# A mixture-of-experts feed-forward on one core: indirect scatters and gathers issued in pairs, each pair behind the landing of the pair ahead

## What is computed

```python
logits = jax.nn.relu(xf @ Wr1 + br1) @ Wr2 + br2
gates = jax.nn.softmax(logits, axis=-1)
tg, ti = jax.lax.top_k(gates, K)              # K = 2
tg = jax.nn.softmax(tg / K, axis=-1)
out = jax.nn.silu(xf @ Ws1 + bs1) @ Ws2 + bs2
for e in range(E):                            # E = 8
    h = jax.nn.silu(xf @ We1[e] + be1[e]) @ We2[e] + be2[e]
    w = jnp.sum(tg * (ti == e), axis=-1)
    out = out + w[:, None] * h
...
x = x + jnp.tanh(g_ffn[1]) * _L1_ffn_ref(_layernorm(x, axis=-1), ...)
```

## Time and profile before

| | |
|---|---|
| three timed runs | 319.92, 322.65, 322.99 us; median 322.65 us |
| the profiled execution, its own time | 319.63 us |
| its span (first to last instruction in the trace) | 317.9 us, so 1.7 us lie around it |
| mean granted TensorE clock | 0.946 |
| busy: PE, DVE, ACT, POOL | 84%, 61%, 49%, 30% |
| indirect DMAs: scatters (L652), gathers (L664) | 16 and 16 |

### The profile page before, as it was taken

How to read it: one execution, slowest core, us unless ns; L and a number is a source line. 1 busy time by engine, 2 the same in 40 slices (tenths; PEclk the granted TensorE clock), 3 DMA queues, 4 the chain that set the end, 5 groups by cost and what they waited for, 6 DMA issues and landing times.

```text
span 317.9 us, 6233 instructions
## 1 busy us (share of the span) xinstructions
PE 268.3 (84%) x2073; PEld 231.7 (73%) x2073; DVE 192.8 (61%) x614; ACT 154.9 (49%) x374; POOL 93.9 (30%) x140
## 2 busy tenths in 40 slices
PE   1998986989989988899999999586798975799960
PEld 0577855778868777798988997574788964799950
DVE  2789836688899975347777487865445730122232
ACT  3582466778876666213342441602559620356420
POOL 1265012578854341021002010550100720035053
PEclk9999999899999999989999999787799995999995
DMA  7799885000000000100000000066800148943132
GB/s 194 250 314 243 217 176 118 1 4 5 26 2 2 3 0 2 36 2 0 0 2 0 2 1 0 20 214 163 276 19 2 41 152 278 278 113 87 34 92 66
DMA packets 30847, 27.31 MB, mean 86 GB/s; under 512 B 2705, under 2 KB 24329, under 8 KB 30816
## 3 DMA queue, kind: packets, MB, share of 16 engines
q1 hardware_dynamic: 29408, 24.45, 26.7%
q0 software_dynamic: 1408, 2.46, 3.1%
HBM read 19.17 MB, written 7.73 MB: 85 GB/s over the span
## 4 chain that ended last, share of the span: by engine, by line
PE 52%; DVE 19%; issue 12%; POOL 8%; DMA 4%; SPq 3%; ACT 2%; POOLq 0%; DVEq 0%; ACTq 0%
PE bank L1386 12%; PE bank L1361 6%; PE bank L1373 5%; PE bank L1194 4%; PE bank L1196 4%; PE bank L1195 3%; PE bank L1179 3%; POOL p_sb L625 3%; DVE xhat_sb L895 3%; DVE sum_sb L832 3%; PE bank L1139 2%; DMA ctx_tok_sb<-in_ctx 2%; PE bank L1150 2%; POOL w_q_sb L664 2%; DVE x_sb L1119 2%
## 5 line engine op out<-in xcount | busy, mean ns | idle before, releaser
L779 ACT ACTIVATE p_sb<-bank,bias_t_sb 128x128 f32<-128x128 f32 x120 | 33.8, 374 | 32.5 <-PE bank L1361 32.4
L625 POOL TENSOR_TENSOR p_sb<-p_sb,recip_sb 128x480 f32<-128x480 f32 x32 | 31.6, 988 | 52.1 <-DVE recip_sb L835 52.1
L768 ACT ACTIVATE hT_sb<-bank,cols_sb 128x512 f32<-128x512 f32 x40 | 27.1, 690 | 40.5 <-PE bank L1196 40.3
L1373 PE MATMUL bank<-we_sb,p_sb 128*128 x240 | 32.3, 280 | 3.5 <-issue 3.5
L673 POOL TENSOR_TENSOR rstd_sb<-veps_sb,minus_half_sb 128x4 f32<-128x4 f32 (+1 forms) x11 | 10.6, 966 | 83.1 <-DVE veps_sb L887 82.9
L1386 PEld LDWEIGHTS bank<-w_sb,hT_sb 128*128 128x128 f32 x256 | 32.0, 200 | 2.1 <-issue 1.3
L1373 PEld LDWEIGHTS bank<-we_sb,p_sb 128*128 128x128 f32 x240 | 29.6, 195 | 4.9 <-issue 4.8
L1386 PE MATMUL bank<-w_sb,hT_sb 128*128 128x128 f32 x256 | 32.8, 284 | 0.0
L1119 DVE SCALAR_TENSOR_TENSOR x_sb<-bank,wts_sb,x_sb 128x128 f32<-128x128 f32 x64 | 18.0, 344 | 19.3 <-PE bank L1386 19.2
L652 POOL DMA_INDIRECT xs_hbm<-xhat_sb,slots_sb x16 | 15.7, 983 | 40.9 <-DVE slots_sb L809 36.7
L1150 PE MATMUL bank<-ident_sb,p_sb 128*120 128x128 f32 x128 | 20.2, 285 | 7.7 <-POOL p_sb L625 7.4
(11 more groups left out here) (221 smaller groups left out, 590.6 us busy)
## 6 DMA issues: line engine op xcount, KB each, us to landing
xs_hbm<-col_rows_sb SPq DMA_DIRECT2D x2, 2048.0 KB, 19.6
tile_w_sb<-in_L_ffn_We SPq DMA_DIRECT2D x15, 256.0 KB, 3.6
w_sb<-in_L_ffn_We SPq DMA_DIRECT2D x8, 256.0 KB, 4.0
w_after_sb<-in_L_ffn_We SPq DMA_DIRECT2D x7, 256.0 KB, 3.7
w_kv_sb<-in_L_xattn_w_kv SPq DMA_DIRECT2D x2, 512.0 KB, 6.6
w_sb<-in_L_ffn_w SPq DMA_DIRECT2D x1, 1024.0 KB, 10.9
xs_sb<-xs_hbm SPq DMA_DIRECT2D x15, 64.0 KB, 2.8
w_kv_sb<-xs_hbm SPq DMA_DIRECT2D x15, 64.0 KB, 2.9
```

Of the source, the lines that this page charges most:

```text
L625: nc.gpsimd.tensor_tensor(p0[j % 4], p0[j % 4], recip0[:, j % 2, :].unsqueeze(2) .broadcast_to([128, HG, SK]), ALU.mult).then_inc(probs_re ...
L768: nc.scalar.activation(hT[:, u % 2, c, :], ps(item)[:, :], ACT.Relu if n == 1 else ACT.Silu, bias=cols[:, col:col + 1]).then_inc(read(item ...
L779: last = nc.scalar.activation(hT_t[:, u % RING, c, :], ps(item)[:, 128 * c:128 * (c + 1)], ACT.Silu, bias=bias_t[:, p, c, j:j + 1])
L1373: last = nc.tensor.matmul(dst[:, 0:C], hT_t[:, slot, c, :], we2[:, bass.ds(e, 1), c, :].rearrange("p a h -> p (a h)"), start=(c == 0), sto ...
```

## The change

Two waits are added on POOL, and nothing else. In the scatter of block i > 0, POOL waits until the scatters of all blocks before it have landed. In the gather of block i > 0, POOL waits until both gathers of block i-1 have landed. Within a pair (k = 0, 1) nothing waits. That is 3 waits in each of the four sequences of 8 indirect DMAs.

```diff
@@ -648,6 +648,8 @@
                     if i == 0:
                         pool.wait_ge(slots_ready, p + 1)
                         pool.wait_ge(loaded["xs_clear"], 32)
+                    else:
+                        pool.wait_ge(scattered[p], 16 * 2 * i)
                     for k in range(2):
                         pool.indirect_dma_start(
                             out=xs_hbm[p], out_offset=bass.IndirectOffsetOnAxis(
@@ -660,6 +662,8 @@
                     for i in range(HB):
                         if p:
                             pool.wait_ge(gathered[i], 16 * 2)
+                        if i:
+                            pool.wait_ge(gathered[i - 1], 16 * 2 * (p + 1))
                         for k in range(2):
                             pool.indirect_dma_start(
                                 out=y_of[p][:, k, i, :], out_offset=None, in_=ys_hbm[p],
```

## The result

The changed kernel is slower: median 331.48 us over four runs (329.56 to 332.09) against 321.51 (319.92 to 322.99). The ratio is 1.030, 95% interval 1.023 to 1.038. The forecast was 330.4 in 325.0 to 335.5. A later series gave the same again: 330.71 against 321.88, ratio 1.030, interval 1.023 to 1.037.

What follows compares the result with a forecast made beforehand. A chain of waits bounds it, the last gather's landing delaying the end one for one. 5.4 + 2.3 + 1.6 = 9.3 gives 328.9 us from the profiled execution's 319.63, 332.0 from the median 322.65; middle 330.4, range 325.0 to 335.5.

Steps and rivals of the forecast that it cites:

- The tail: Half 1's gathers at the kernel's end: three waits delay the last gather and the end one for one, +5.4 us.
- the restart behind a landing: Time POOL needs to start its next DMA after a waited-for landing: taken as 0.5 us, ends 0.3 and 0.77.
- Half 0's start: Half 0's scatters: SP's row loads start 3.7 us later, less 2.05 of slack, so +1.6 us.
- The slack: At half 0's start, PE and DVE had other work, so 2.05 us of later rows would be hidden.
- Half 1's start: Half 1's scatters: SP waits 3.2 us longer, row loads land 0.9 faster, PE starts +2.3 us late.
- Half 0's gathers: Last gather issued 5.3 us later, but covered by DVE's later combine and 4.65 us idle behind it: 0.
- The clock: Rival, 0.11: each longer PE idle leaves one more block at half clock, 2 x 1.75 = +3.5 us.
- Only the tail shows: Rival, 0.14: the scatters' six waits are hidden, only half 1's gathers cost, +5.4: 325.0 or 328.1 us.
- Not slower: Rival, 0.02: POOL's 0.94 us per indirect DMA is queue back-pressure, so issues get shorter: 318.3 or 321.3 us.
- Waits that do nothing: Rival, 0.03: landings are over when POOL comes to the waits, so time as before.

Runs made afterwards that it cites:

- e1_gather1: Kernel before plus only the three waits between the pairs of half 1's gathers, two semaphores each: 331.81 us, ratio 1.018.
- f4_gather0_late: Kernel before with half 0's gathers, no waits between them, starting only when tile 8 of half 1 is copied out: 322.33 us, ratio 1.001.
- f3_gather0_again: Kernel before plus only the three waits between the pairs of half 0's gathers, run again on another chip: 322.74 us, ratio 1.002.
- f1_before: Kernel before, unchanged, run once more with a profile: 322.58 us, ratio 1.001.
- e3_scatter1: Kernel before plus only the three waits between the scatter pairs of half 1: 331.08 us, ratio 1.012.
- e7_gather1_each: Kernel before, each half 1 gather waiting for the one ahead, one semaphore each; waits for half 0's gathers moved ahead of all eight: 337.14 us, ratio 1.037.

## Why the prediction was right, point by point

**The tail: right place, mis-sized (+5.4, measured +6.7 and +6.4).** All of it reaches the end: DVE's last combine starts 2.5 to 2.6 us behind the last gather before and after. Alone it costs 1.8% (`e1_gather1`). The term that was off is the restart behind a landing: 0.5 was taken between the ends 0.3 and 0.77. It is 0.7 here, because these waits carry two semaphores, and 0.2 to 0.3 with one. The nearest row, 0.7 behind a store's landing, had the size; whether its three semaphores were the reason, as the prediction half suspected, was not tested apart. The other part is the first landing, 3.2 us (2.9 in the second profile) instead of 2.7: DMA issues at 310.70 us and then 315.86 us of the changed kernel:

```profile
w_q_sb<-ys_hbm,y_slots_sb POOLq DMA_INDIRECT x1, 3.2
...
w_q_sb<-ys_hbm,y_slots_sb POOLq DMA_INDIRECT x1, 2.5
```

**Half 0's start: right mechanism, too small (+1.6, measured +2.5).** The last scatter was predicted to land 3.7 us later, and SP's first row load came 3.9 later (17.66 us behind the first scatter instead of 13.77). The wait beside the weight loads was longer, 4.7 us instead of the 3.5 taken, and the restarts shorter, 0.2 to 0.3 instead of 0.5, which nearly cancels. What wasn't in the sum: the fourth row load took 2.6 us, not 1.8. DMA issues at 210.90 and at 221.04 us of the changed kernel:

```profile
xs_hbm<-xhat_sb,slots_sb POOLq DMA_INDIRECT x1, 4.7
...
xs_sb<-xs_hbm SPq DMA_DIRECT2D x1, 64.0 KB, 2.6
```

3.9 + 0.8 - 2.05 of slack = 2.65, against 2.5 measured. The slack, read from when PE and DVE would have been free, was right.

**Half 1's start: right, a little too large (+2.3, measured +1.6).** The restart was 0.3, so a step between pairs is 2.51 and not 2.7; the last landing took 3.4 as against 3.5 taken; SP was 2.5 late, not 3.2. That the row loads then land 0.9 us faster came true: 1.9 instead of 2.8. PE's idle grew from 5.18 to 6.72, where about 7.5 was expected.

**Half 0's gathers: right (0).** The last lands at 303.3 and DVE's combine starts at 306.54; `f4_gather0_late` shows that even 10.7 us are covered by the combine and the idle behind it.

**The clock: a rival by itself, in fact a part.** One microsecond lies behind half 1's first multiplications, and both profiles of the changed kernel have it. PE's timeline of the changed kernel, the next two tiles' worth behind 271.89:

```profile
273.74 1.92 PE L1377 MATMUL bank<-we_sb,p_sb 128*128 x8
275.44 1.70 PE L1365 MATMUL bank<-pT_sb,w_sb 128*128 128x128 f32 x8
276.97 1.06 PE L1377 MATMUL bank<-we_sb,p_sb 128*128 x8
```

In the kernel before the first two of these blocks took 1.56 and 1.06:

```profile
269.16 1.56 PE L1373 MATMUL bank<-we_sb,p_sb 128*128 x8
270.55 1.06 PE L1361 MATMUL bank<-pT_sb,w_sb 128*128 128x128 f32 x8
```

PE stood at 1.2 GHz (granted 0.50 in 272 to 276 us) for 1 us longer. But `f3_gather0_again`, with an idle of 5.70 us and none of the scatter waits, shows 1.92 and 1.82 as well, and `f1_before`, with 7.60 us, only 1.92 and 1.17, so the longer idle isn't shown to be the cause: when the clock comes back also varies between executions. At half 0's start nothing was added, the 16 matmuls took 3.58 us instead of 3.48. The prediction's "+1.75 for each" was too much.

**The rivals that fell.** Only the tail shows: no, half 0's and half 1's stages grew in both profiles of the changed kernel, and half 1's in `e3_scatter1` alone. Not slower, by quicker issues: an indirect DMA took 0.94 to 0.96 us of POOL behind a wait as before it (the first scatters of a sequence 1.0 to 1.1 in both kernels), and with one in flight in `e7_gather1_each` 0.94 to 1.00. Waits that do nothing: true only of waits two pairs back.

The terms' errors, +1.3, +0.9, -0.7 and the +1.0 of the clock, add up to 2.5 of the 3.0 us between 12.3 and 9.3; the rest is the 0.4 ahead of the first scatter and rounding. The time was still near the middle of the range since it started from halfway between the own time and the median.

That the forecast came so near is in part luck. The medians differ by 10.0 and 8.8 us, which the sum's 9.3 matches, while the stages grew by 11.9 us against an execution at the fast end. The terms were too small by about as much as that execution lay below the usual one. Where a usual execution of the kernel before spends the 2 to 3 us isn't settled. The stage to half 1's first gather may be the place: it took 36.6 us in the first profile, 40.6 in `f1_before` and 41.3 in `f3_gather0_again`, which differs from it only in the gathers of half 0, but 37.6 in both profiles of the changed kernel.

The Trainium skill (DMA: Bandwidth & Descriptors, "Anatomy of one DMA") puts most of a DMA's fixed cost of about 2 us into the receipt of the write, before which its semaphore can't rise. The runs fit that as far as they go: the gathers' 2.5 us stayed 2.5 with two in flight and, but for the first, 2.4 to 2.6 with one; they don't show the receipt by itself. The estimate by the page's formula, 2.15 us for 64 KB, was too low for these gathers and near the 2.2 of the scatters.

## What to carry to other kernels

A wait for a landing in a queue of small indirect DMAs costs the landing plus the restart less one issue step, here 1.25 us for the scatters (3.7 beside the weight loads), and for the gathers 2 to 2.7 with two semaphores and 1.4 to 1.7 with one. It is paid in full where the last of them ends the kernel, in part where an engine or a queue behind it has slack, and not at all where the work beside it is longer. Waiting two pairs back instead of one bounds what is in flight and cost nothing here, where a landing takes 2.5 us and 3.75 us lie between a pair's second gather and the pair after the next. Before pricing such a wait on GpSimd, count the semaphores on the instruction: the second one costs as well when it blocks.

## What was not expected of the hardware

- POOL restarts 0.2 to 0.3 us behind a landing with one semaphore to wait for and 0.7 us with two, when the last one blocks; fulfilled waits cost nothing (steps stay at 1.25 us).
- A scatter beside five 256 KB loads took 4.6 and 4.7 us to land in the two profiles of the changed kernel, one beside little traffic 2.2.
- The same kernel took 321.9 us in the median on one chip and 325.3 to 327.7 on another. On the second, PE stood idle for 1.6 to 2.5 us, or crept through single matmuls with holes of 0.2 to 1.6 us, beside three of the four sequences of eight indirect DMAs wherever these had no waits, and not beside those with waits, in eight profiles; on the first in none of four. Beside the fourth it was DVE that came 1.3 us late. The cause is open.
- In some executions the first second-weight multiplications of half 1 waited 3.8 us instead of 1.8 and PE fell to half clock behind it (`f1_before`, `f3_gather0_again`): their profiled executions took 326.20 and 322.86 us, those without it 319.63 (the first profile of before) and 320.08 (`f4_gather0_late`). In these four it goes with the longer times; that it makes up the spread of one kernel's runs over 320 to 326 us isn't shown.
